# Router logits of a mixture layer taken relative to expert 7: seven PSUM banks per tile in place of eight half-width groups, weight differences made on GpSimd

## What is computed

```
logits = (h @ router_w.T + router_b).reshape(T, O, E)     # T 4096, O 512, E 8
probs = softmax(logits, axis=-1)
w, sel = top_k(probs, 2)
w = w / sum(w)                                            # per token and output column
c = zeros((T, E)).at[t, sel].add(w)                       # summed over the 512 columns
expert_out = einsum('th,eoh->teo', h, expert_w) + expert_b
final = einsum('te,teo->to', c, expert_out)
```

## Time and profile before

| | before |
|---|---|
| median of 3 runs | 2306.94 us |
| span of the profiled execution | 2306.4 us |
| TensorE busy | 2285.2 us (99%) |
| VectorE busy | 1682.9 us (73%) |
| ScalarE busy | 1145.2 us (50%) |
| GpSimd busy | 11.3 us |
| share of TensorE in the chain that ended last | 89% |

### The profile page before, as it was taken

One profiled execution on the slowest core, in us unless ns is written; L12 is line 12 of the kernel. 1 busy time (PEld: TensorE's weight loads), 2 busy tenths in 40 slices (PEclk: granted clock), 3 DMA queues, 4 the chain that ended last, 5 costly groups with the idle time before them and its releaser, 6 DMA issues.

```text
span 2306.4 us, 29968 instructions
## 1 busy us (share of the span) xinstructions
PE 2285.2 (99%) x10201; PEld 1881.0 (82%) x10201; DVE 1682.9 (73%) x2522; ACT 1145.2 (50%) x1686; POOL 11.3 (0%) x20
## 2 busy tenths in 40 slices
PE   7999999999999999999999999999999999999999
PEld 5777888888888887888888888888888888888887
DVE  8985444444434346888899999998988888888883
ACT  7754333232323235788888888888422222222221
POOL 0000000000000000000000000000000000000000
PEclk9999999999999999999999999999999999999999
DMA  6314212122121317211111212115322222222220
GB/s 206 105 42 139 76 37 75 55 56 75 37 86 26 91 37 255 73 57 66 59 64 64 78 55 77 61 58 199 134 96 82 77 95 79 80 95 76 83 82 23
DMA packets 154026, 191.04 MB, mean 83 GB/s; under 512 B 62898, under 2 KB 96242, under 8 KB 151666
## 3 DMA queue, kind: packets, MB, share of 16 engines
q1 hardware_dynamic: 110690, 135.26, 18.1%
q10 hardware_dynamic: 43152, 55.06, 7.3%
q0 software_dynamic: 128, 0.07, 0.0%
HBM read 129.01 MB, written 61.34 MB: 83 GB/s over the span
## 4 chain that ended last, share of the span: by engine, by line
PE 89%; issue 5%; DVE 4%; ACT 2%; DMA 0%; ACTq 0%; POOLq 0%; POOL 0%; DVEq 0%; SPq 0%
PE slot L1599 16%; PE plane L1749 10%; PE plane L1747 10%; PE plane L1745 10%; PE ex L1785 10%; PE ex L1787 10%; PE ex L1786 10%; PE pj L1612 7%; PE slot L1661 3%; PE slot L1568 1%; PE slot L1650 1%; DVE cols L1238 1%; DVE ew_lo L1478 1%; ACT x1t_hi L795 0%; PE slot L1578 0%
## 5 line engine op out<-in xcount | busy, mean ns | idle before, releaser
L1599 PE MATMUL slot<-y_hi,wgu 128*128 128x512 f32 x1024 | 402.6, 393 | 1.4 <-DVE y_lo L1118 0.7
L1599 PE MATMUL slot<-y_lo,wgu 128*128 128x512 f32 x1024 | 399.8, 390 | 0.0
L1745 PE MATMUL plane<-rw_hi,hb 128*128 128x512 f32 x1008 | 392.2, 389 | 0.0
L1749 PE MATMUL plane<-rw_lo,hb 128*128 128x512 f32 x1008 | 392.1, 389 | 0.0
L1747 PE MATMUL plane<-rw_hi,hb 128*128 128x512 f32 x1008 | 392.1, 389 | 0.0
L1785 PE MATMUL ex<-ew_hi,hb 128*128 128x512 f32 x992 | 386.0, 389 | 0.2 <-ACT ex L1056 0.2
L1787 PE MATMUL ex<-ew_lo,hb 128*128 128x512 f32 x992 | 385.9, 389 | 0.0
L1786 PE MATMUL ex<-ew_hi,hb 128*128 128x512 f32 x992 | 385.9, 389 | 0.0
L1056 ACT ACTIVATE ex<-eb_sb 128x512 f32<-128x512 f32 x248 | 149.0, 602 | 448.9 <-DVE acc L1507 385.8
L1453 DVE SCALAR_TENSOR_TENSOR lead_in<-code_in,wts 128x1024 bf16<-128x1024 bf16 x256 | 311.4, 1216 | 1.2
L1599 PEld LDWEIGHTS slot<-y_hi,wgu 128*128 128x128 f32 x1024 | 192.8, 188 | 45.5 <-DVE q_scale L1125 2.9
(11 more groups left out here) (164 smaller groups left out, 3213.6 us busy)
## 6 DMA issues: line engine op xcount, KB each, us to landing
hb<-h_scratch SPq DMA_DIRECT2D x34, 512.0 KB, 3.3
code_scratch<-half_code SPq DMA_DIRECT2D x64, 256.0 KB, 2.0
half_in<-code_scratch SPq DMA_DIRECT2D x32, 512.0 KB, 3.4
hb<-h_scratch ACTq DMA_DIRECT2D x30, 512.0 KB, 3.7
h_scratch<-ht ACTq DMA_DIRECT2D x48, 256.0 KB, 2.9
q_raw<-in_w_ffn SPq DMA_DIRECT2D x21, 512.0 KB, 3.5
x_scratch<-x_res ACTq DMA_DIRECT2D x8, 1024.0 KB, 4.3
rraw<-in_rwT SPq DMA_DIRECT2D x8, 1024.0 KB, 9.2
```

Source lines behind the costliest of these rows:

```text
L1599: last = mm(slot[s % 2][:, g, :], wgu[:, c, r * P:(r + 1) * P], y[:, c, :], start=(c == 0 and v == 0), stop=(c == DC - 1 and v == 1))
L1745: mm(bank[:, :, :], hb[:, u, c, 0, :], rw_hi[:, w, c, o], start=False, stop=False, skip_group_check=True)
L1749: last = mm(bank[:, :, :], hb[:, u, c, 0, :], rw_lo[:, w, c, o], start=False, stop=True, skip_group_check=True)
```

## The change

The router's weights and biases are replaced by their differences to those of expert 7, whose logit is then 0 everywhere and needs no matmul. GpSimd makes the weight differences (`relative(c)`, 28 pieces of 128x512, each fetched from DRAM, subtracted and sent to DRAM scratch on GpSimd's own queue) between its `power` steps, and one subtraction over 128x3584 for the biases. A tile now has 7 groups of 12 matmuls, one per expert, all 512 columns, each with a bank of its own. The tournament runs once per whole tile over 7 planes and a constant 0, with `tops` and `lows` three planes wide, and joins the codes of the tile before. The 36 early pieces start at tile 7, one after an even and two after an odd tile. The last tile's tournament is spread between the `expert` steps of expert tile 1.

```diff
-PT = 8
-KT = 12
+PT = E - 1
+KT = 15
+NS = 3
...
+            def relative(c):
+
+                o = slice(c * D, (c + 1) * D)
+                pool.dma_start(base, rwT[E - 1][:, o]).then_inc(base_in, 16)
+                for e in range(PT):
+                    k = c * PT + e
+                    if k:
+                        pool.wait_ge(rel_stored, 16 * k)
+                    pool.dma_start(rel[:, :], rwT[e][:, o]).then_inc(rel_in, 16)
+                    pool.wait_ge(base_in, 16 * (c + 1))
+                    pool.wait_ge(rel_in, 16 * (k + 1))
+                    nc.gpsimd.tensor_tensor(rel[:, :], rel[:, :], base, ALU.subtract).then_inc(rel_done, 1)
+                    pool.wait_ge(rel_done, k + 1)
+                    pool.dma_start(rel_dram[e][:, o], rel[:, :]).then_inc(rel_stored, 16)
+
             power(0)
-            with pool.Fori(1, NBLK - 1) as i:
-                power(i)
+            power(1)
+            for c in range(DC):
+                power(2 + c)
+                relative(c)
+            power(NBLK - 2)
+            pool.wait_ge(braw_in, 16)
+            nc.gpsimd.tensor_tensor(bias_sb[:, 0:PT, :], bias_sb[:, 0:PT, :],
+                                    bias_sb[:, E - 1, :].unsqueeze(1).to_broadcast([P, PT, D]), ALU.subtract).then_inc(bias_rel, 1)
             power(NBLK - 1)
...
             def router(n, u):
-                evacuate(n, 0)
+                evacuate(n, u, 0)
+                if not (isinstance(n, int) and n < 2):
+                    for q in range(4):
+                        place(n - 2, q)
+                for e in range(1, PT - 1):
+                    evacuate(n, u, e)
                 if not (isinstance(n, int) and n == 0):
-                    stand(n - 1, 1)
-                evacuate(n, 1)
-                if isinstance(n, int) and n == NT - 2:
-                    for b in range(4):
-                        seed_spare(b)
-                stand(n, 0)
+                    sign_of_second(n - 1, mb[:, :], "m2")
+                    sign_of_four(n - 1, 1 - u)
+                evacuate(n, u, PT - 1)
+                if not (isinstance(n, int) and n == 0):
+                    sign_of_three(n - 1, 1 - u)
...
+            for n in range(7, NT - 1):
+                router(n, n % 2)
+                for slot_of_tile in range(1 + n % 2):
                     if early:
...
             def router(n, u, trip):
-                for s in range(2):
-                    for b in range(4):
-                        group(n, u, trip, s, b)
+                for e in range(PT):
+                    group(n, u, trip, e)
...
+            dve.wait_ge(signs, NS * (NT - 1))
             for e in range(E):
                 expert(0, e, 0, 0)
-            join(NT - 1, 0)
+            join(NT - 2)
             dve.wait_ge(eb_in, 16)
             dve.wait_ge(exp_step, E)
             for e in range(E):
                 bias(e)
             for e in range(E):
                 expert(1, e, 1, 0)
-                if e == 2:
-                    half(NT - 1, 1, 1, NT // 2 - 1, joins=False, scratch=late_work)
-            join(NT - 1, 1)
-            for n in range(2, 4):
-                tile(n, n, n // 2)
+                for step in range(2 * e + 1, 2 * e + 3):
+                    tournament(NT - 1, 1, step, scratch=late_work)
+            tile(2, 2, 1)
+            join(NT - 1)
+            tile(3, 3, 1)
```

More of the change, by code:

```diff
@@ L281, in build @@
         res = sb("res", [P, 2, D], F32, p3)
+        late_mb = sb("late_mb", [P, D], F32, p3)
         p3.close()
[L283 to L287, removed]
[L288 to L292 removed]
+        L = sb("L", [P, 2, PT, D], F32, p2)
+        lead = sb("lead", [P, 2, D], F32, p2)
+        p3 = ExitStack()
+        late_top = sb("late_top", [P, 3, D], F32, p3)
+        late_low = sb("late_low", [P, 3, D], F32, p3)
+        p3.close()
+        sgn = sb("sgn", [P, E * D], BF16, p2)
+        code = sb("code", [P, 4, D], U16, p2)
+        bank = [pb(f"bank{s}", [P, D], p2) for s in range(E)]
         p2.close()
[L296 to L298 removed]
+        plane = bank[4:8] + bank[0:3]
+        ex = bank[3:4] + bank[4:8] + bank[0:3]
         pbc.close()
@@ L558, in load_halves, with tiles @@
             def load_halves(n):
[L559 to L573, removed]
+                sp.dma_start(half_in[:, :, :].bitcast(BF16).rearrange("p q n -> p (q n)"), one(code_dram, n)).then_inc(half_in_done, 16)
+            for n in range(2):
+                sp.wait_ge(plane_filled, (n + 1) * PT)
+                load_h(2 + n, n)
+            sp.wait_ge(lead_ready, 1)
+            spill_lead(0, 0)
+            def tiles(m):
+                left = [sp.snap(m * (2 * PT) + (u + 1) * PT) for u in range(2)]
+                joins = [sp.snap(m * 2 + (u - 1)) for u in range(2)]
+                leads = [sp.snap(m * 2 + u) for u in range(2)]
+                for u in range(2):
+                    sp.wait_ge(plane_filled, left[u])
+                    load_h(m * 2 + (2 + u), u)
+                    sp.wait_ge(joined, joins[u])
+                    spill_code(m * 2 + (u - 2))
+                    sp.wait_ge(lead_ready, leads[u])
+                    spill_lead(m * 2 + (u - 1), 1 - u)
+            with sp.Fori(1, 3) as m:
+                tiles(m)
+            sp.wait_ge(code_out, 16)
+            load_halves(0)
             for u in range(2):
@@ L576, in _ @@
                 load_lead(u, u)
-            for s in range(2):
[L578 to L589, removed]
+            with sp.Fori(3, 5) as m:
                 tiles(m)
@@ L941, in _ @@
             adapt(NBLK - 1)
-            for b in range(1, 4):
-                seed(0, b)
+            for e in range(1, 4):
+                seed(e)
             split_router(3)
@@ L1446, in total, with router @@
+            def router(n, u, joins=True):
+                for step in range(1, 13):
+                    tournament(n, u, step)
+                if joins:
+                    join(n - 1)
+                for step in range(13, 17):
+                    tournament(n, u, step)
             def total(n, e, k):
@@ L1764, in _ @@
             linear(NBLK - 1, 1)
-            for s in range(2):
-                for b in range(4):
-                    if s or b:
-                        group(0, 0, 0, s, b, first=True)
+            for e in range(1, PT):
+                group(0, 0, 0, e, first=True)
             router(1, 1, 0)
@@ L1773, in _ @@
                 router(m * 2 + 2, 0, m + 1)
-            for b in range(4):
-                group(NT - 1, 1, NT // 2 - 1, 0, b)
-                group(NT - 1, 1, NT // 2 - 1, 1, b, bank=spare[b])
+            router(NT - 1, 1, NT // 2 - 1)
             def experts(m, u):
```

363 lines of the change are left out of this document (204 added, 159 removed).

## The result

The changed kernel takes 2227.74 us, the median of 4 runs (2225.1 to 2232.13), and the kernel before 2307.48 in runs beside it (4 runs, 2306.49 to 2308.06). The ratio is 0.9656, with a 95% interval of 0.9644 to 0.9667: 3.4% faster. The forecast was 2222.4 with a range of 2218 to 2238. Direction and range hold; the gain is about 80 us in place of 84.5.

The account below looks back on a forecast made before the run. TensorE was taken to bound the kernel, busy 99% of the span. 2306.9 - 87.0 (removed matmuls) + 2 (bias subtraction) + 0.5 (small VectorE waits in the blocks) = 2222.4 us, range 2218 to 2238.

Parts of the forecast that it names:

- TensorE's term: Router tiles: 384 matmuls removed at 0.2265 us each, 87.0 us saved.
- Rivals 1 and 6: VectorE bounds tiles with early pieces, 2235 us (chance 0.13); ScalarE or VectorE needs the old tile time, no gain (0.02).
- VectorE per tile: Router tiles: VectorE needs 16.3 us, at most 16.6, and stays hidden behind TensorE's 19.03 us.
- Waits inside the tile: Router tiles: some tenths of a us of VectorE wait in the join, costed at nothing.
- GpSimd's chain: Blocks: fetch, subtraction and store, 11 us a piece; seven take 78 of 108 us between power steps, hidden.
- rivals 3 and 4: GpSimd's chain outlasts a block: 17 us a piece gives 2267 us (chance 0.10); 19.5 gives 2334, slower (0.03).
- I take 2: A block's feed-forward steps: GpSimd's bias subtraction over 3584 columns holds VectorE's two-input instructions, costing 2 us.
- The upper bound of 5.6: Bias subtraction: one low part held whole, less its cover, 7.5 + 0.6 - 2.5 = 5.6 us.
- The sign to look for: At 856 to 866: idle time up to 7 us before `hid_lo` or `sumsq`, one TensorE wait of 1 to 5 us.
- The step that failed: Blocks: each weight subtraction may hold VectorE up to 1.4 us, covered by 2.5 us before TensorE needs the low part.
- The hand-over: Router to experts: weights arrive each 2.46 us, the last with three us to spare, all hidden, no cost.
- rival 2: The hand-over stalls through slower last fetches or a stuck first x1 fetch; 8 us late gives 2228 us; chance 0.12.

Follow-up runs that it names:

- the doubled step: The changed kernel with step 1 of the tournament (1536 columns) done twice in each of tiles 7 to 30: 2253.37 us, ratio 0.9769.
- the worst place: The changed kernel with the bias subtraction held back until VectorE is about to make a low part in block 7: 2231.19 us, ratio 0.967.
- the hold removed: Two versions of the changed kernel: bias subtraction as seven instructions of 512 columns, 2224.54 us; or cut to 8 columns of one expert, 2224.76 us.
- the base: The changed kernel run again unaltered, its trace being the second profile: 2227.23 us, ratio 0.9652.

## Why the prediction was right, and where it was off

**TensorE's term.** 384 x 0.2265 = 87.0 us; the router stretch gives 87.1, without a gap. Rivals 1 and 6 didn't happen.

**VectorE per tile.** Forecast 16.3 us, at most 16.6. One tile of the changed kernel, VectorE in order of time:

```profile
1237.10 1.75 DVE L1481 TENSOR_TENSOR tops<-L 128x1536 f32<-128x1536 f32 x1
1238.77 1.75 DVE L1483 TENSOR_TENSOR lows<-L 128x1536 f32<-128x1536 f32 x1
...
1242.24 0.68 DVE L1496 SCALAR_TENSOR_TENSOR mb<-L,tops 128x512 f32<-128x512 f32 x1
1242.85 0.68 DVE L1498 SCALAR_TENSOR_TENSOR tops<-L,tops 128x512 f32<-128x512 f32 x1
...
1247.12 1.22 DVE L1437 TENSOR_TENSOR code<-sgn 128x2048 uint16<-128x2048 uint16 x1
1248.25 0.68 DVE L1513 TENSOR_TENSOR mb<-ma,lows 128x512 f32<-128x512 f32 x1
...
1253.45 1.22 DVE L1539 SCALAR_TENSOR_TENSOR lead_in<-code_in,wts 128x1024 bf16<-128x1024 bf16 x1
```

1253.45 - 1237.10 = 16.35 us. The line of 0.067 + 0.533 us for each 512 columns, taken from two widths, gave 1.67 for 1536 columns (1238.77 - 1237.10) and 1.14 for the join (measured 1.13); fused instructions lie 0.61 apart. That this margin was real and thin is what the doubled step shows: 42 us more work, 26 more time.

**Waits inside the tile.** Forecast at nothing, though waits in the join were seen coming. They came, larger than the "some tenths" (14 waits for `sgn`, 15.1 us in all, the longest 4.3), and cost TensorE nothing.

**GpSimd's chain.** Forecast 11 us a piece. Measured are 8 to 12, on average 9.1 (the first block's seven fetches start from 349.16 to 403.55). Seven are done with 47 to 49 us to spare before the next power step, so rivals 3 and 4 were far off. Both DMAs were overpriced: fetch and store land 3.4 and 2.6 us after issue, where 5 and 5 were taken from the 16 KB ones of the earlier trace rows, issued at the program's start.

**The bias subtraction.** The step "I take 2" was the right mechanism with a size that is only one of its values. Duration 8.24 us, inside 7 to 10; the estimate of 7.9 from the Trainium skill (GPSIMD Engine Reference, Elementwise — side-by-side cycle accounting) is 4% short of it. Its cost was 2.6 us in the profiled execution, 4.2 where the clock fell behind the same wait, and 7.5 at the worst place. The upper bound of 5.6 covers the 4.5 us that TensorE waited there and lacked the clock. Medians with the hold removed (2224.5 and 2224.8) put it at 2.5 to 2.7, with intervals that overlap the base's. The sign to look for was given as idle time before `hid_lo` or `sumsq`; the hold stood in the duration instead.

**The step that failed** is "VectorE may be held for up to one subtraction, 1.4 us; [...] 2.5 us later, which covers that". The cover was read at a low part in the middle of a step, where it is 2.5 us. Ahead of the turned rows there is none: TensorE waits there already, 0.5 us in each block of the kernel before. So each hold at that `sumsq` goes straight through, 1.1 us a block, in two blocks of the first profile and four of the second. The sum had 0.5 us for all blocks; the first profile has 2.5. Without the small subtractions every full block is back at 109.0 to 109.2.

**The hand-over.** "Three us to spare" took 2.46 us as the pace of each weight. The sixth came 10 us after its issue, behind the code on the same queue, and the hand-over cost 1.3 us. That is rival 2 in small, by a transfer of the code that had no term in the sum.

**The rest.** Holds and hand-over are 5.2 + 1.3 = 6.5 us in place of 2.5: 4 of the 5.3 us by which the median missed. The largest share of the rest, 1.1 us, is the base. The trace of before, span 2306.4, was of an execution with the slow start of 0.96 and 0.90. Every run on record is timed 1.6 to 1.8 us above its own span, so that execution took about 2308.1 and not the 2306.9 that the sum began from; a sum made in the trace can't be read against the median as it stands. The median of the changed kernel also lies 0.3 us above its profiled execution. No errors offset each other to bring the total into the range: the big term was right, and the three small ones (bias 2.6 for 2, blocks 2.5 for 0.5, hand-over 1.3 for 0) were all too low.

## What to carry to other kernels

Work given to an idle engine is free only at the places where the engine that it can hold has slack: look for the wait that already exists (here 0.5 us at the turned rows), not for an average cover. Where GpSimd and VectorE both read SBUF, cut GpSimd's long instruction into short ones: here it took 28% longer itself and left TensorE no wait for `hid_lo`. And when a tile is made shorter for one engine, price the next engine by distances between starts: in the tiles with early pieces VectorE had 15 / 24 = 0.6 us a tile left.

## What the runs showed of the hardware

A hold between VectorE and GpSimd is seen in the held instruction's duration (8.41, 7.82, 1.78 in place of 0.69 us), so that no idle time of VectorE names it; only TensorE's wait for what stands behind it, or for the held result itself, does. With GpSimd's work cut into seven, VectorE's instructions get in between two pieces and last 0.98 to 1.77 us.

TensorE's granted clock after a short idle time is not settled by that time's length alone. In a wait of 4.5 us it fell to 0.50 and stayed there for some 5.5 us of matmuls; after one of 2.2 us it fell for some 3 us in one execution and stayed at 1.00 in others of nearly the same kernel. What decides it is open. It makes one and the same wait cost 2.6 or 4.2 us, and the changed kernel's highest runs (2231 to 2232, mean clock 0.998 where others have 0.999 or 1.0) fit such a fall, which was not profiled in them.
